# Two-layer graph network kernel on one core: each Z bank of a tile signals its own last matmul, and ScalarE waits for that signal instead of the count matmul's

## The reference, cut to what matters

```
h   = relu(layernorm(x))                                    # x: 1250 x 512
W_r = sum_b w_comp[r,b] * bases[b]                          # 32 relations, 8 bases
x   = x + segment_sum(ew[e] * (h[src[e]] @ W_type[e]), dst) + h_bias    # 40000 edges, sorted by dst
h   = relu(layernorm(x))
deg = out-degree of each node, its own loop included;  dis = rsqrt(deg)
u   = h @ W.T + b
x   = x + relu(segment_sum(dis[src] * dis[dst] * u[src], dst, loops included))
```

## Time and profile before

| | |
|---|---|
| runs (3) | 599.51, 600.43, 601.35 us; median 600.43 us |
| profiled execution | 597.75 us, of it 596.0 us span in the trace |
| PE busy | 495.9 us (83%), 5873 matmuls |
| DVE, ACT, POOL busy | 343.8, 155.7, 355.9 us |
| L1722, narrow matmuls | 301.8 us, 4020 |
| L804, gathers | 336.0 us, 335 |
| L936 and L938, first copy of a bank | 80 |
| L1366, low part of a bank | 72 |

### The profile page before, as it was taken

How to read it: one execution, slowest core, us unless ns; L and a number is a source line. 1 busy time by engine, 2 the same in 40 slices (tenths; PEclk the granted TensorE clock), 3 DMA queues, 4 the chain that set the end, 5 groups by cost and what they waited for, 6 DMA issues and landing times.

```text
span 596.0 us, 16021 instructions
## 1 busy us (share of the span) xinstructions
PE 495.9 (83%) x5873; PEld 313.3 (53%) x5873; DVE 343.8 (58%) x999; ACT 155.7 (26%) x280; POOL 355.9 (60%) x476
## 2 busy tenths in 40 slices
PE   3040667899998999999999998998989999999973
PEld 1020655555665656666556656655656565664530
DVE  8984674587845456857756765664566333132036
ACT  3682452444211122202320320320232101131020
POOL 3635656577776767756757757767767777730000
PEclk9565777999999999999999999999999999999985
DMA  8798968666787877876966868878868888745016
GB/s 283 240 354 307 362 218 318 187 183 180 225 242 211 264 241 216 258 220 174 278 200 172 279 180 230 275 205 255 261 198 238 264 235 254 231 143 160 0 24 153
DMA packets 51861, 132.84 MB, mean 223 GB/s; under 512 B 11775, under 2 KB 17776, under 8 KB 51702
## 3 DMA queue, kind: packets, MB, share of 16 engines
q0 software_dynamic: 27040, 99.60, 55.6%
q1 hardware_dynamic: 23788, 30.99, 16.5%
q10 hardware_dynamic: 954, 1.13, 0.6%
HBM read 123.14 MB, written 11.10 MB: 225 GB/s over the span
## 4 chain that ended last, share of the span: by engine, by line
PE 59%; DVE 12%; DMA 10%; issue 7%; POOL 6%; ACT 3%; SPq 1%; DVEq 0%; ACTq 0%
PE PS L1752 24%; PE PS L1722 19%; DMA gath<-rows_layer,srcs 8%; POOL gath L804 5%; PE PS L1744 5%; PE PS L1793 4%; PE PS L1772 4%; DMA types_by_slot<-h_t 1%; DVE stats L1075 1%; PE PS L1728 1%; DVE room_b L1366 1%; DVE room_b L1558 1%; PE PS L1761 1%; DVE gath L1572 1%; DVE room_c L1058 1%
## 5 line engine op out<-in xcount | busy, mean ns | idle before, releaser
L804 POOL DMA_INDIRECT gath<-rows_layer,srcs x335 | 336.0, 1003 | 156.3 <-PE PS L1728 78.5
L1722 PE MATMUL PS<-sel,gath 128*128 128x48 f16 (+7 forms) x4020 | 301.8, 204 | 31.7 <-issue 12.0
L1722 PEld LDWEIGHTS PS<-sel,gath 128*128 128x128 f16 x4020 | 237.3, 101 | 160.7 <-issue 73.5
L1752 PE MATMUL PS<-room_b,zt 128*128 128x512 f16 x384 | 127.1, 380 | 0.1
L1752 PE MATMUL PS<-room_b 128*128 128x512 f16 (+1 forms) x384 | 117.1, 380 | 1.2 <-issue 0.6
L1728 PE MATMUL PS<-oh_ad,gath 128*128 128x30 bf16 (+7 forms) x335 | 64.2, 192 | 1.9 <-DVE c_i L1369 1.9
L1793 PE MATMUL PS<-u_t,room_c 128*128 128x512 f16 (+2 forms) x200 | 57.8, 397 | 6.6 <-issue 3.6
L873 ACT CAST val<-val_f 128x64 f16<-128x64 f32 x42 | 11.0, 262 | 174.4 <-DVE val_f L1245 174.4
L1276 DVE TENSOR_TENSOR masks<-iota_n,dloc 128x24 bf16<-128x24 f32 (+12 forms) x92 | 17.7, 193 | 62.6 <-issue 36.4
L1752 PEld LDWEIGHTS PS<-room_b 128*128 128x128 f16 (+1 forms) x384 | 38.4, 105 | 13.6 <-issue 0.9
L1282 DVE TENSOR_TENSOR sel<-masks,val 128x192 f32<-128x192 bf16 (+12 forms) x92 | 38.7, 421 | 0.0
(11 more groups left out here) (245 smaller groups left out, 488.2 us busy)
## 6 DMA issues: line engine op xcount, KB each, us to landing
room_b<-in_L_gnn_bases_dram SPq DMA_DIRECT2D x8, 1024.0 KB, 10.8
gath<-rows_layer,srcs POOLq DMA_INDIRECT x335
x_base<-in_x_dram SPq DMA_DIRECT2D x5, 500.0 KB
x_t<-x_base SPq DMA_DIRECT2D x19, 128.0 KB
u_t<-in_x_dram SPq DMA_DIRECT2D x9, 256.0 KB, 5.9
types<-types_by_slot SPq DMA_DIRECT2D x144, 16.0 KB
x_layer<-x_t SPq DMA_DIRECT2D x18, 128.0 KB, 4.5
gath<-x_layer SPq DMA_DIRECT2D x18, 128.0 KB, 2.7
```

The lines of the kernel that those rows point to most:

```text
L804: pool.indirect_dma_start(out=gath[:, s % UN, :], out_offset=None, in_=tab0_d[:, :], in_offset=bass.IndirectOffsetOnAxis(ap=srcs[:, s:s + ...
L1722: mm(there, gath[:, s % UN, D * t + P * f:D * t + P * (f + 1)], sel_parts[:, here, k, 0:NB * w, u], start=first and t == 0 and u == 1, sto ...
L1752: last = mm(PS[0:r, PBANK[q], :], zt[q][:, t, f, b, 0:r], base_hl[:, b, u, f, :], start=(m == 0), stop=(m == NM - 1))
```

## The change

At the last slot of a tile, the third narrow matmul into each Z bank increments a new semaphore, `s_zdone`. ScalarE waits for that signal before each of the four copies, in place of one wait for the count matmul. VectorE's wait for the count matmul, so far only in pair 0 and ahead of everything, now stands in every tile, right before it copies the counts.

```diff
+        s_zdone = sem("s_zdone")
...
-                act.wait_ge(s_used, LAST[r] + 1)
                 for f in range(FT):
+                    act.wait_ge(s_zdone, FT * r + f + 1)
                     if q == 0:
                         a.copy(z_whole[:, f, :, TN * h:TN * (h + 1)], zbank(f)).then_inc(s_hi, 1)
                     else:
...
-                if q == 0:
-                    dve.wait_ge(s_used, LAST[r] + 1)
                 for f in range(FT if q else 0):
                     hi, lo = (zt[q][:, s, f, :, TN * h:TN * (h + 1)] for s in range(2))
                     dve.wait_ge(s_hi, FT * r + f + 1)
                     v.scalar_tensor_tensor(lo, zbank(f), ZDOWN, hi, ALU.mult, ALU.subtract).then_inc(s_lo, 1)
                 if r:
                     dve.wait_ge(s_cst, 2 * r)
+                dve.wait_ge(s_used, LAST[r] + 1)
                 v.tensor_copy(c_i[:, 0, :], PS[:, CB, 0:HA * TN]).then_inc(s_ci, 1)
...
-                        mm(there, gath[:, s % UN, D * t + P * f:D * t + P * (f + 1)], sel_parts[:, here, k, 0:NB * w, u],
-                           start=first and t == 0 and u == 1, stop=True, skip_group_check=True)
+                        last = mm(there, gath[:, s % UN, D * t + P * f:D * t + P * (f + 1)], sel_parts[:, here, k, 0:NB * w, u],
+                                  start=first and t == 0 and u == 1, stop=True, skip_group_check=True)
+                    if s == LAST[r]:
+                        last.then_inc(s_zdone, 1)
```

## The result

The changed kernel takes 592.76 us (median of 6 runs, 589.36 to 594.36), the kernel before 599.97 us (6 runs, 598.49 to 602.04). The ratio is 0.9891 with a 95% interval of [0.9863, 0.9920]: 6.5 us faster [4.8, 8.2]; the two medians lie 7.2 us apart. The forecast was 4.4 us faster. All ratios here are of fast runs: four of the 34 runs of the kernel before that stood beside the first four experiments were slow ones, one of them at 2141 us, and are left out.

What follows compares the result with a forecast made beforehand. TensorE's losses at tile-end flushes bound the kernel, with POOL's gathers (1.25 us each) second. Tile-end gains summed to 4.4 us after gather discounts, signals and waits at 0: 600.4 - 4.4 = 596.0 us, range 594.6 to 597.6.

Steps and rivals of the forecast that it cites:

- Nothing at tiles 0, 4 and 16: Tile 0: ScalarE busy until 78.08; tiles 4 and 16: no flush loss, or a gather wait; no gain at these ends.
- Signals and further waits at 0: 80 signalling matmuls, four ScalarE waits instead of one and VectorE's moved wait were each taken to cost 0 us.
- Tile 7's gain given back whole: At tile 7's end 0.52 us lead, 0.46 lost; POOL runs unbroken from gather 113, TensorE waits for gather 127: nothing kept.
- Rival 2: No effect: another wait ends last everywhere, so ScalarE gets no earlier start; 600.4 us, chance 0.12.
- rival 4: Gathers meet SyncE's transfers in another phase and land 0.8 us later at eight waits; slower, 602.4 us, chance 0.07.
- rival 3: Semaphore signals on the matmuls serialize, costing 0.10 us per tile end; 598.1 us, chance 0.05.
- Rival 1: More gains lie before near-waits for gathers, so about half of 4.4 us is left; 598.2 us, chance 0.20.
- The earlier signal: At each tile end the gain is the smaller of bank 0's usable lead and TensorE's loss; 5.4 us with nothing discounted.
- Tile 14: At its end ScalarE goes from the layer norm straight into the copies (373.19 + 0.81 against 373.92): no gain.
- Tile 12: Its end loses nothing at the flush, or TensorE waits for a gather there: no gain.
- Tile 6 was halved: At tile 6's end gain 0.54 us, half counted, 0.27, since gather 113 started 1.75 us after its release.
- Tile 1's half: At tile 1's end gain 0.46 us, half counted, 0.23, since TensorE had just waited for late gather 24.

Runs made afterwards that it cites:

- the first four experiments: Against the kernel before: early signals with the old wait 600.15 us; early waits at tiles 0-3 598.63, tiles 4-19 593.40; one wait for the last Z bank 599.26.
- the first four tiles: Kernel before with ScalarE's early waits at tiles 0 to 3 only, later tiles waiting for the count matmul: 598.63 us, ratio 0.9993.

## Why the prediction was off in size

**What held.** The mechanism (ScalarE's start in tile 6 0.53 us earlier against the count matmul, bank 0's lead). The tile ends that the forecast gave a gain: 5.4 us in its list before anything was taken off, 5.6 measured. Nothing at tiles 0, 4 and 16. Signals and further waits at 0. Tile 7's gain given back whole (below). The stretch from gather 265 to 330, which has no tile end in it, took what it did. Rival 2 (no effect) and rival 4 (landings, slower) are refuted by the time, rival 3 (signals) by the traces. Rival 1 had a mechanism that is real, gains lost again at gathers, but its size, 2.2 us left, lies outside the interval.

**What the page on signals gave.** The Trainium skill, "TensorE: Matmul & The Clock Gate", section "The cost: per-tile semaphore tail", has increments serialize at 26.3 ns each where every matmul of a burst signals, an estimated 2.1 us here. This case does not agree: 0.00 to 0.02 us for the four signals of a tile end. They are 0.15 to 0.35 us apart here, not on successive matmuls; which of the two makes the difference was not tried.

**What failed: the step "The earlier signal", which put four tile ends and everything behind the low parts on VectorE at nothing.** These terms measured 2.6 us, and with them the list should have been 8.2 us, not 5.4. What the gathers took of it was about 2 us, not the 1.0 taken off; this second error has the other sign and hid part of the first. The items:

- *Zeros read from one execution.* Tile 14 was counted at nothing, since ScalarE went from the layer norm straight into the copies at 373.19. That holds for that execution only: with the old wait ScalarE sat idle there for 0.79 to 1.84 us in the three other traces. The timelines of PE and ACT there with signals alone (old wait), and then with the change in tiles 4 on:

```profile
369.83 0.81 ACT L967 ACTIVATE h_t<-x_t,nmr,rstd 128x512 f32<-128x512 f32 x1 [0.43 <-DVE nmr L1434]
...
370.20 0.20 PE L1722 MATMUL PS<-sel,gath 128*128 128x64 f16 x1 [0.50 <-DMA gath<-rows_layer,srcs]
...
371.43 0.19 PE L1730 MATMUL PS<-oh_ad,gath 128*128 128x40 bf16 x1
...
371.72 2.06 ACT L939 ACTIVATE room_b<-PS 128x512 f16<-128x512 f32 x4 [1.07 <-PE PS L1730]
```

```profile
371.04 0.20 PE L1725 MATMUL PS<-sel,gath 128*128 128x64 f16 x1 [1.34 <-DMA gath<-rows_layer,srcs]
...
372.64 2.06 ACT L942 ACTIVATE room_b<-PS 128x512 f16<-128x512 f32 x4 [0.45 <-PE PS L1725]
...
373.30 0.19 PE L1733 MATMUL PS<-oh_ad,gath 128*128 128x40 bf16 x1
```

  TensorE waits for a gather in one of the last slots, the layer norm is over before the banks are complete, and ScalarE sits idle for 1.07 us with the old wait. With the new one it starts 0.66 us before the count matmul. Gain 0.57, in all three new traces. Tile 12 (0.2 to 0.5), tile 2 (0.16) and tile 18 (0.1 to 0.5, behind gather 330) were zeros too. The four make 1.5 us.

- *A term that was missing.* I followed the low parts to TensorE but not what stands behind them on VectorE. The count copy is earlier by the same half microsecond, and so is all that VectorE does next. Where TensorE waits for one of these, it gains: 0.37 us in the second slot of tile 5, whose own head gained nothing (the load of window words behind the wait for the count copy), 0.24 at slot 167 (the edge values), 0.21 and 0.3 at slots 216 and 332. Together 1.1 us.

- *Discounts for gathers, one wrong and one right.* Tile 6 was halved because gather 113 started 1.75 us after its release "for a reason that I can't see". That distance is 1.75 us in all ten traces, so the gain passes whole: from tile 6's last count matmul to slot 127's, over the ends of tiles 6 and 7, the new executions are 0.6 us shorter by their means, which is tile 6's 0.53. (What fixes the distance stays open.) Tile 7 was "given back whole", and it was: from tile 7's last count matmul to slot 127's the four old executions took 17.4 to 18.3 us and the three new ones 17.6 to 18.0, the same by their means, although the tile's end is 0.50 shorter. POOL works without a stop from gather 113 to gather 127 and takes 17.5 to 17.7 us for it in ten traces of ten. Another such place was not in the forecast: in two of the three new traces slot 182 waits 0.85 and 1.13 us for its gather, where it waited 0.30 to 0.68 with the old wait, and in the third TensorE lost time just ahead of it. Tile 1's half can't be settled: 0.5 in the trace, but the time of the first four tiles doesn't resolve it.

Added up, the local gains are 8.2 us. Of these 6.4 lie between slot 49 and gather 265, where the stretch is shorter by 4.5; 0.7 us show behind gather 330, and 1.1 us are the ends of tiles 1, 2 and 3, which lie ahead of slot 49. That makes about 6.3, close to the 6.5 measured, so about 2 us are given back at the gathers. How much each single item carries to the end is not settled: executions of one kernel differ by over 2 us in the same stretch.

## What to carry to other kernels

A zero that rests on a near-miss in one trace (ScalarE 0.1 us late at tile 14) is not a zero; look at a second execution, above all where transfers jitter. When a releaser moves earlier, follow everything that its engines do after it, down to the register loads of the waiting engine. A stretch in which the gathers never pause swallows a gain whole, as between gathers 113 and 127, and one that opens with a release passes it on. And look for work that an engine does ahead of a flush and could as well do behind it: moving the two split steps was worth 2.6 us more by the medians.

## What the runs showed of the hardware that I had not expected

- Signals on matmuls 0.15 to 0.35 us apart cost 0.00 to 0.02 us per tile end (four signals), with 80 of them in the kernel.
- With a load of words into TensorE's registers behind a wait, the first matmul that hangs on it (slot 64) starts 1.14 to 1.15 us after the end of the count copy waited for; the matmuls still in the queue don't cover all of that, and 0.41 us of idle time are left in the kernel before. With the load moved away the pause is gone.
- The granted clock fell to 0.83 in one execution in a stretch where another had 1.00 (110 to 120 us), with nothing changed in the instructions there but the waits and signals; some 3 us, as much as half of the change. In the changed kernel's second profiled execution the slots of that stretch took 23.9 us, not 26.8.
